# A GNN layer on one core: all eight node tiles normalised on ScalarE with the relu in the same instruction

## The reference

```python
h = maximum(layernorm(x), 0)                      # (x - mean) / sqrt(var + 1e-5), then relu
m = relu(concat(h[src], h[dst], edge_attr) @ Wm1 + bm1)
m = relu(m @ Wm2 + bm2)
agg = segment_sum(m, dst, N)
u = relu(concat(h, agg) @ Wu1 + bu1)
out = x + h + (u @ Wu2 + bu2)
```

## Time and profile before

| | |
|---|---|
| median of 3 runs | 810.18 us (807.91 to 810.64) |
| the profiled execution's own time | 810.81 us |
| its span | 809.1 us |
| granted TensorE clock, share of full | 0.996 |
| busy: TensorE, VectorE, ScalarE, GpSimd | 690.6, 694.9, 613.3, 564.5 us |
| L371 on VectorE | 392 tiles of xg, 49 of xn |
| L422 on ScalarE | 343 tiles of xn |

### The profile page before, as it was taken

The page is one execution under the profiler, slowest core; times in us unless marked ns, Lnnn a source line. Parts: engine busy times, 40 slices in busy tenths (PEclk is TensorE's granted clock), DMA queues, the critical chain, the costliest instruction groups (busy, mean ns, idle before and its releaser), DMA issues. The chain is left out here.

```text
span 809.1 us, 19398 instructions
## 1 busy us (share of the span) xinstructions
PE 690.6 (85%) x3158; PEld 416.5 (51%) x3159; DVE 694.9 (86%) x2407; ACT 613.3 (76%) x1384; POOL 564.5 (70%) x783
## 2 busy tenths in 40 slices
PE   0589888888888888888888888769999999999997
PEld 0344444444444444444444444435777787777775
DVE  2989988888888888888888888749999999898886
ACT  0588777777777777778777777656677999888886
POOL 7777777777777777777777777418977666555543
PEclk9999999999999999999999999999999999999999
DMA  6466666666666666666666666540478999999998
GB/s 144 124 211 216 215 214 208 204 201 202 198 214 206 214 213 190 207 209 212 214 211 211 207 205 208 201 156 1 132 216 270 330 330 344 366 350 346 360 356 309
DMA packets 99727, 184.56 MB, mean 228 GB/s; under 512 B 15101, under 2 KB 16512, under 8 KB 99700
## 3 DMA queue, kind: packets, MB, share of 16 engines
q1 hardware_dynamic: 46084, 80.64, 29.8%
q10 hardware_dynamic: 41072, 77.93, 27.3%
q0 software_dynamic: 12544, 25.72, 12.8%
HBM read 107.25 MB, written 76.98 MB: 228 GB/s over the span
## 5 line engine op out<-in xcount | busy, mean ns | idle before, releaser
L240 POOL DMA_INDIRECT xg<-x_in,ends_all x392 | 392.6, 1002 | 120.1 <-DMA xg<-x_in,ends_all 104.6
L637 POOL TENSOR_TENSOR low<-msgs,high 128x128 fp32r<-128x128 f32 x303 | 153.9, 523 | 71.9 <-ACT high L717 68.5
L666 DVE TENSOR_SCALAR hot<-node,dst_f,minus_base 128x512 fp32r<-128x512 f32 x229 | 130.6, 614 | 23.7 <-issue 16.3
L770 PE MATMUL bank<-hot,low 128*128 128x512 f32 x303 | 137.4, 454 | 10.8 <-DVE hot L666 7.0
L422 ACT ACTIVATE zn<-xn,shift,rstd 128x128 f32<-128x128 f32 x343 | 141.8, 483 | 1.6 <-DVE shift L345 1.2
L497 PE MATMUL bank<-ident,xg 128*128 128x128 f32 x392 | 64.7, 289 | 89.7 <-DVE xg L371 89.7
L302 DVE BATCH_NORM_STATS2 bn<-xg 128x6 f32<-128x128 f32 x392 | 80.5, 278 | 53.2 <-DMA xg<-x_in,ends_all 53.1
L771 PE MATMUL bank<-hot,high 128*128 128x512 f32 x303 | 120.9, 399 | 0.0
L504 PE MATMUL bank<-ht,w_uh 128*128 128x512 f32 x196 | 108.3, 634 | 10.6 <-ACT ht L434 9.2
L429 ACT ACTIVATE ht<-bank 128x512 f32<-128x512 f32 x196 | 109.9, 592 | 6.3 <-DMA xh_scratch<-xh_o 2.0
L497 PEld LDWEIGHTS bank<-ident,xg 128*128 128x128 f32 x392 | 41.8, 142 | 139.9 <-issue 109.9
(11 more groups left out here) (75 smaller groups left out, 1007.7 us busy)
## 6 DMA issues: line engine op xcount, KB each, us to landing
hu_scratch<-ht ACTq DMA_DIRECT2D x49, 512.0 KB
xh_scratch<-xh_o ACTq DMA_DIRECT2D x49, 512.0 KB
hu_i<-hu_scratch SPq DMA_DIRECT2D x98, 256.0 KB, 4.4
xh_i<-xh_scratch SPq DMA_DIRECT2D x98, 256.0 KB, 4.5
out<-xh_o SPq DMA_DIRECT2D x97, 256.0 KB, 4.4
xn<-x_in ACTq DMA_DIRECT2D x44, 512.0 KB
xg<-x_in,ends_all POOLq DMA_INDIRECT x392
edge<-edge_t_in ACTq DMA_DIRECT2D x45, 64.0 KB
```

Of the source, the lines that this page charges most:

```text
L240: pool.indirect_dma_start(xg[:, slot, t, :], None, x, bass.IndirectOffsetOnAxis(ap=ends_all[:, s, t:t + 1], axis=0), engine_sem=s_made).th ...
L637: return pool.tensor_tensor(low[:, at, :], msgs[:, k, :], high[:, at, :].bitcast(F32), ALU.subtract)
L666: return dve.tensor_scalar(hot[:, at, :], node[:], dst_f[:, bass.ds(k, 1)], minus_base[:, bass.ds(g, 1)], ALU.subtract, ALU.is_equal)
L770: pe.matmul(to, low[:, at, :], hot[:, at, :], start=start, stop=False, skip_group_check=True)
```

## The change

ScalarE normalises all eight node tiles, with ACT.Relu in place of ACT.Identity, so zn holds h instead of its value before the relu. VectorE normalises the eight tiles of xg alone, and `x_plus_h` adds zn and xn with no maximum. The relu on the transposes (L429) stays. The semaphore counts follow: s_zv counts two parts a step, TensorE's transposes of zn wait for s_za alone, and VectorE's waits for s_zv before it overwrites zn and for s_xs before it normalises go.

```diff
-            VECTOR_TILES = 9
-            assert 8 < VECTOR_TILES < 12
-
...
                     if at_least(s, 2):
                         dve.wait_ge(s_za, 2 * (s - 1))
-                        dve.wait_ge(s_zv, 3 * (s - 1))
+                        dve.wait_ge(s_zv, 2 * (s - 1))
...
-                    dve.scalar_tensor_tensor(
-                        out=xh_o[:, half, h, :].rearrange("p (j d) -> p j d", j=4), in0=zn[:, half, 4 * h:4 * h + 4, :],
-                        scalar=0.0, in1=xn[:, slot, 4 * h:4 * h + 4, :], op0=ALU.max, op1=ALU.add).then_inc(s_xs, 1)
+
+                    dve.tensor_tensor(xh_o[:, half, h, :].rearrange("p (j d) -> p j d", j=4),
+                                      zn[:, half, 4 * h:4 * h + 4, :], xn[:, slot, 4 * h:4 * h + 4, :], ALU.add
+                                      ).then_inc(s_xs, 1)
...
                         dve.wait_ge(s_tr, 4 * (s - 1))
-                        dve.wait_ge(s_xs, 2 * (s - 1))
-                    for t in range(VECTOR_TILES):
-                        if t < 8:
-                            of = to = xg[:, slot, t, :]
-                        else:
-                            of, to = xn[:, slot, t - 8, :], zn[:, slot % 2, t - 8, :]
-                        ins = dve.tensor_scalar(to, of, mean[:, slot % 2, t:t + 1], rstd[:, slot % 2, t:t + 1],
-                                                ALU.subtract, ALU.mult)
-                        if t in (3, 7, VECTOR_TILES - 1):
+                    for t in range(8):
+                        ins = dve.tensor_scalar(xg[:, slot, t, :], xg[:, slot, t, :], mean[:, slot % 2, t:t + 1],
+                                                rstd[:, slot % 2, t:t + 1], ALU.subtract, ALU.mult)
+                        if t % 4 == 3:
                             ins.then_inc(s_zv, 1)
...
                             dve.wait_ge(s_za, 2 * (s - 1))
-                            dve.wait_ge(s_zv, 3 * (s - 1))
...
-                            ins = act.activation(zn[:, prev % 2, t - 8, :], xn[:, prev, t - 8, :], ACT.Identity,
+                            ins = act.activation(zn[:, prev % 2, t - 8, :], xn[:, prev, t - 8, :], ACT.Relu,
                                                  bias=shift[:, prev % 2, t:t + 1], scale=rstd[:, prev % 2, t:t + 1])
...
-                        normalise(range(VECTOR_TILES, 12))
+                        normalise(range(8, 12))
...
-                        pe.wait_ge(s_zv, 3 * s + min(q, 2) + 1)
-                        if q >= 2:
+                        if q < 2:
+                            pe.wait_ge(s_zv, 2 * s + q + 1)
+                        else:
                             pe.wait_ge(s_za, 2 * s + q - 1)
```

## The result

The changed kernel takes 807.84 us (median of 20 runs, 805.32 to 810.3) against 809.7 us for the kernel before in the same set (20 runs, 807.37 to 811.9). The ratio is 0.9973, with a 95% interval of 0.9963 to 0.9984: faster by 0.27%, some 2 us. The forecast was 810.2 us and no change. The time lies in the range, and the gain is smaller than the 0.3% that I had called distinguishable, but its interval excludes no change. So the forecast missed a small true gain, and the question is which step it comes from.

The account below looks back on a forecast made before the run. GpSimd's stream of gathers plus a drain was taken to bound stage one, stage two being unchanged. All terms summed to 0 us against the median of 810.18, so 810.2 us, range 803 to 815.

Parts of the forecast that it names:

- GpSimd's stream: Stage one: 49 steps of eight gathers, 10.5 us each, 514 us, set its length together with a drain.
- ScalarE did not become the bound: Rival on ScalarE's normalisations through relus: a step grows to 10.71 us, 10 us slower, 821 us; chance 0.07.
- the pair's 1.28 us: VectorE's two plain additions, read as 0.64 us each against 688 ns for x + h: 0 to 0.05 us shorter each.
- The waits go together: Step on the removed semaphore waits of VectorE and TensorE: nothing gained on the path, and the drain costs 0.
- The line on x + h: VectorE's sum as plain addition: its start does not move; 0 taken, 2.5 us at the utmost.
- the other half of the mechanism: Inference that VectorE's two-input sums hold up two of a step's eight gathers: 0.53 us a step, 26 us in all.
- the sum: All parts of the change added for the whole kernel: 0 us, so 810.2 us; chance of no change 0.74.
- two other bounds: Allowances in the range: 2.5 us for the sums' end on VectorE, some 2 us for the catch-up at the start.
- My own sign of being wrong: Test on GpSimd's gathers: wrong if their mean moves from 1.00 us by 0.01 or more, 4 us.
- The rival of kinder collisions: Later sums on VectorE free a gather: 0.23 us a step, 799 us, or 2 us in the catch-up; chance 0.12.
- The port rival: VectorE's tensor_scalars hold descriptor writing back; one fewer frees up to 0.26 us a step, 13 us, 797 us; chance 0.02.
- The drain: End of stage one after the last gather: stays near 24.9 us, with 0.6 us to spare on ScalarE, cost 0.

Follow-up runs that it names:

- e1: Changed kernel with VectorE's wait for s_zv put back just ahead of the first sum of x and h; ratio to the kernel before 0.9994.
- e3: Changed kernel with the old instruction for x + h (maximum with 0, then add) kept; ratio to the kernel before 0.9956.
- e2: Kernel before with only the wait for s_zv moved from ahead of the first sum to the beginning of the step; ratio to the unmoved kernel 0.9950.
- e6: Changed kernel with the sums x + h and additions of b_out replaced by one-input tensor_scalars, leaving x and b_out out; ratio to the kernel before 0.9901.
- e9: Repeat of e2's kernel, with no further edit, beside the changed kernel on one chip; ratio to the kernel before 0.9962.
- e4: Changed kernel with both sums of x and h one place earlier, the eighth bn_stats behind them; ratio to the kernel before 1.0126.
- e5: Changed kernel with two, five or seven redundant satisfied waits ahead of the first sum; ratios to the kernel before 0.9983, 1.0003 and 0.9999.

## Why the prediction was right and wrong

**Right.** GpSimd's stream sets stage one, and nothing else does: its waits are the same. The removed normalisation is worth 0 (hidden by the wait for the rows, which rose from 1.33 to 1.62 us), and so is the added activation (482 ns each; the wait of 0.39 us ahead of L471 shrank to 0.2, the 1.18 us ahead of sd stayed, at 1.23). The plain addition takes 688 ns as before. ScalarE did not become the bound. e1 tests these three together: 0.9994. One reading was off without effect: an addition of b_out takes 0.68 us and starts 0.60 behind the one before it, so the pair's 1.28 us do not make 0.64 each. That they are each nothing rests on e3 for the addition; the tile and the activation were not tried apart.

**Wrong: "The waits go together".** That step asked only who would be released earlier, and priced the removals at nothing. It named VectorE's wait for its older sums (s_xs) and left out the one that mattered, the wait for s_zv just ahead of the first sum; the section on the change calls it a wait before VectorE overwrites zn, but at this place it guards the reading of zn. The line on x + h then said that "the start of the sum does not move". It moves. A satisfied wait ahead of the first sum cost 0.07 to 0.09 us of VectorE's issue time (0.18 to 0.10 us from r2 to the sum; e1: 0.165). That it shows at this place, perhaps because the instruction ahead of it is a small one of 16 columns, was not tested; at the beginning of the step, where VectorE waits for the rows anyway, it costs nothing (e2). The prediction had the other half of the mechanism, as an inference: the seventh gather is held until the first sum lets it go. By that, 0.07 us a step goes straight into the bound, 49 x 0.07 = 3.4 us, against 2.9 us in the sum of the gathers and 2.2 at the last landing. The term was missing from the sum. That the time still fell into the range is no merit of the sum: the range had room for two other bounds, 2.5 us for the end of the sums and 2 us for the catch-up, each about as large as this gain. My own sign of being wrong, a mean gather 0.01 us off, was set too wide for it: it moved by 0.008, from 1002 to 994 ns.

**The rival of kinder collisions** had the right coupling and the wrong direction: I had the sums getting later through ScalarE in the catch-up, down to 0.94 us for the seventh gather. They got earlier, by one wait, and the gather is held for a shorter time rather than missed.

**The port rival** was refused on the ground that gathers beside the tensor_scalars take 0.94 us. Those rows were too few. After the change the first gather of a step takes 1.06 in some steps (347.21 above) and 1.00 in the mean, and e6 shows the hold outright. Both gathers in the rows begin less than 0.1 us into a tensor_scalar. The removed ninth tensor_scalar brought nothing all the same, as e2, which keeps it, has the full gain.

**The drain** was put at no change; 27.2 us against 24.9 in one execution each, of which 0.9 us is the end of the last gather. Whether the rest came through the change is open: in the twelve other profiles, e2 and e9 without the change among them, it lies between 25.3 and 26.9 us. The granted clock of TensorE between 515 and 540 us was 1.00 before and 0.86 after, but also 1.00 in e3, whose drain takes 26.2 us.

## What to carry to other kernels

On an engine whose work others collide with, a satisfied wait need not be free: price it as issue time (0.07 to 0.09 us here), and keep such waits at a place where the engine waits anyway. Where an engine with slack can hold up the one that is the bound, look at when its instructions start, not only at how long they take: 0.07 us a step came through here and 0.33 us of removed work did not. Before moving code to exploit such an alignment, find the release rule from a few timeline rows; by estimate alone e4 lost 1.3%. Even with the rule, seven waits meant to push the sums behind the gather brought nothing (e5), as the landing no longer fixed their place.

## What was not expected of the hardware

An indirect gather issued from GpSimd takes 0.94 us, or, if it begins within certain instructions of VectorE, until 0.94 us after a point in them: 0.57 us after the start of a two-input addition of 512 columns, 0.35 us after that of a tensor_scalar of 512 columns (e6), 0.21 us after that of one of 128. A bn_stats does not hold it. Through this a semaphore wait of some 0.08 us, satisfied and with 1.3 us of slack behind it on its engine, is visible in the device time.
